# One core's adapter kernel: sixteen transposes and a whole down product in a row, gathers a group further ahead, one of four A copies on VectorE, A loaded in 512-byte runs

## The chip, the cores and the metric

The kernel runs on one core of a Trainium2 chip. The metric is the device time of one execution in microseconds (us). The kernel before has a median of 96.18 us over three runs (95.92 to 96.72).

## The reference

`x` holds 64 sequences of 64 tokens with 1024 features, in float32. Each sequence names one of 8 adapters (`itok_B_3_7`). An adapter has a `B` of 16 x 1024 (rank by features) and an `A` of 1024 x 16. What is computed:

```python
B_sel = B[adapter_ids]                       # 64 x 16 x 1024
A_sel = A[adapter_ids]                       # 64 x 1024 x 16
Bx    = einsum('bni,bri->bnr', x, B_sel)     # down to rank 16
out   = einsum('bnr,bor->bno', Bx, A_sel)    # up to 1024
return x + out * 1.0
```

So 16.8 MB are read, 16.8 MB are written, and between them every token goes through its sequence's two small products.

## The kernel before, in words

**Tiles and groups.** A tile is 128 tokens (two sequences) by 1024 features. A duo is two tiles, so four sequences, and there are 16 duos. All 32 tiles of x have a place of their own in SBUF (`x_all`), where the result is added in place and stored from. SyncE (SP) issues the load of A, then all loads of x, then the stores in order of tiles. ScalarE issues the loads of B and of the ids.

**Start.** TensorE (PE) does 24 transposes of an identity, then transposes B (L195). ScalarE (ACT) copies it into `b_table` (L287), which has for every adapter and chunk of 128 features a 128 x 16 block. A is split into a rounded part and a rest by VectorE (DVE; L338, L341, L344) and ACT (L294, L296), transposed on PE (`a_unit`, L212) and copied into `a_table` (L306, L348).

**A duo's work.** `transpose_unit` (L221) turns four 128 x 128 chunks of x into one PSUM bank; there are four units in a duo, and ACT copies each into `x_t` (`copy_x`, L301). `down` (L234) multiplies each of the eight chunks with the adapter's block for four sequences, into the 128 rows of a `bx_bank`. ACT rounds the result into `bx_parts` (`split_high`, L316), DVE writes the rest beside it (`split_rest`, L355), and GpSimd (POOL) copies both to the lower 64 rows (`double_parts`, L169). `up` (L254) multiplies that with the adapter's A into `y_banks`, and DVE adds the product to x (`add_x`, L363).

**The gathers.** Which block of the tables a sequence needs is known only at run time. POOL reads the ids into registers (L141) and copies the four blocks of B (`gather_b`, L151) and the four of A (`gather_a`, L162) of each duo into `b_duo` and `a_duo`, which have two buffers each.

**Order.** Every engine has its list written out by hand, and semaphores tie the lists together. PE's loop over the duos is: two transpose units of the next duo, the first half of this duo's down product (chunks 0 to 3), the two other units, the second half, then the up product of the duo before. Transposes use two PSUM banks, down products two, and up products four. In POOL's list a duo has: registers, B of the next duo, A of this one, `double_parts` of this one. The wait for `parts_done` ahead of the B copies is for POOL's own copy just before them.

Of the kernel before, what the change touches and what calls it, by code (L numbers as in the profile page):

```python
# [8 lines left out]
def lora_kernel(nc: bass.Bass, x: bass.AP, ids: bass.AP, a_in: bass.AP, b_in: bass.AP, out: bass.AP):  # L9
# [21 lines left out]
    A_BY_DVE = (0, 2, 4, 6)  # L31
    B_HOME, A_HOME, PARTS_HOME = TILES - 1, TILES - 2, TILES - 6
    B_OWN = CHUNKS * RANK
    WARM_UPS = 24

# [7 lines left out]
    with ctx:  # L43
# [24 lines left out]
        t_bank = [pb(f"t_bank{i}", [P, BANK]) for i in range(2)]  # L68
        bx_bank = [pb(f"bx_bank{i}", [P, BANK]) for i in range(2)]
# [18 lines left out]
        a_gathered = sem("a_gathered")  # L88
# [22 lines left out]

        def own_tokens(duo, first_row, end_row):
# [18 lines left out]
        def _(pool):  # L131
# [8 lines left out]
            def adapters_of(duo):  # L140
                return nc.values_load_multi_w_load_instructions(  # L141
                    id_row[0:1, duo * DUO_SEQS:(duo + 1) * DUO_SEQS], engines=[pool.engine],
                    min_val=0, max_val=ADAPTERS - 1,
                    skip_runtime_bounds_check_because="the ids are indices of the adapters")[1]

            def gather_b(duo, adapters):
# [8 lines left out]
                last.then_inc(b_gathered, 1)  # L155

            def gather_a(duo, adapters):
# [6 lines left out]
                last.then_inc(a_gathered, 1)  # L164
# [8 lines left out]
            here = adapters_of(0)  # L173
            gather_b(0, here)
            for duo in range(DUOS):
                if duo + 1 < DUOS:
                    after = adapters_of(duo + 1)
                    gather_b(duo + 1, after)
                if duo == 0:
# [208 lines left out]
```

## Time and profile before

| | |
|---|---|
| median of three runs | 96.18 us (95.92 to 96.72) |
| profiled execution, device time | 96.29 us |
| its span in the profile | 94.4 us |
| PE busy | 81.5 us (86%) |
| POOL busy | 67.1 us (71%) |
| DVE busy | 58.4 us (62%) |
| ACT busy | 53.1 us (56%) |
| DMA | 34.83 MB, 369 GB/s over the span |

The span runs from the first to the last recorded piece of work. The device time of the same execution is 1.9 us longer. Busy shares are means over a start, a long middle and an end with different limits, so the rows further below are read by stage. PEld is PE's loading of weights, which overlaps its multiplications, and SPq is SyncE's issuing of DMAs.

### The profile page before, as it was taken

Reading aid. Unit: us, or ns where it says so; the run is one execution under the profiler, and the core shown is the slowest. Engines: PE = TensorE matmul, PEld = TensorE weight load, DVE = VectorE, ACT = ScalarE, POOL = GpSimd, SP = SyncE. Lnnn points to the kernel's source line nnn. Section 1 sums busy time; section 2 is a strip of 40 time slices with the busy share of each in tenths; the row PEclk is TensorE's granted clock in tenths of the full one; section 3 lists DMA queues with packets and bytes.
Section 4 is the critical chain, followed back from the end, with each engine's and each line's share of the span. In section 5 each row is a group of like instructions: output and inputs, shape, how many; then the busy total and the mean of one; then the engine's idle time right before and its main releaser. Section 6 shows DMA issues by size and latency. Waiting matters only on the chain.

```text
span 94.4 us, 3723 instructions
## 1 busy us (share of the span) xinstructions
PE 81.5 (86%) x1472; PEld 64.5 (68%) x1472; DVE 58.4 (62%) x105; ACT 53.1 (56%) x138; POOL 67.1 (71%) x152
## 2 busy tenths in 40 slices
PE   3994999999999999899999999999989999652800
PEld 3993998787786768587877787777767877440400
DVE  0009541219696949396969677685857695949760
ACT  2219687985747475657667676757556757110000
POOL 6003906379798999979797979797979798986000
PEclk9999999999999999999999999999999999975555
DMA  1999999999999999999999999999999998664676
GB/s 19 305 294 394 419 417 408 408 408 412 401 413 406 408 403 403 410 412 403 408 413 408 419 403 415 417 412 415 417 410 419 410 380 327 271 266 198 247 318 252
DMA packets 11202, 34.83 MB, mean 369 GB/s; under 512 B 2866, under 2 KB 2866, under 8 KB 11186
## 3 DMA queue, kind: packets, MB, share of 16 engines
q1 hardware_dynamic: 11040, 34.08, 91.7%
q10 hardware_dynamic: 146, 0.52, 1.6%
q8 instruction: 11, 0.18, 0.7%
q14 instruction: 5, 0.04, 0.1%
HBM read 17.83 MB, written 16.78 MB: 367 GB/s over the span
## 4 chain that ended last, share of the span: by engine, by line
PE 69%; POOL 9%; DMA 7%; issue 5%; DVE 4%; POOLq 2%; DVEq 1%
PE t_bank L221 31%; PE bx_bank L234 18%; PE y_banks L254 16%; POOL a_duo L162 7%; DMA x_all<-in_A 7%; PE y_banks L212 4%; DVE x_all L363 1%; DVE x_all L341 1%; POOL b_duo L151 1%; DVEq L43 1%; DVE x_all L338 1%; DVE x_all L344 1%; POOL bx_parts L169 1%; POOLq L43 0%; POOLq L162 0%
## 5 line engine op out<-in xcount | busy, mean ns | idle before, releaser
L363 DVE TENSOR_TENSOR x_all<-y_banks,x_all 128x1024 f32<-128x1024 f32 x32 | 39.1, 1224 | 18.7 <-PE y_banks L254 18.2
L301 ACT COPY x_t<-t_bank 128x512 f32<-128x512 f32 x64 | 34.4, 591 | 19.5 <-PE t_bank L221 19.5
L162 POOL CAST a_duo<-a_table 128x512 fp32r x64 | 36.6, 609 | 3.4 <-ACT a_table L306 3.2
L221 PE MATMUL t_bank<-ident,x_all 128*128 128x128 f32 x256 | 34.9, 279 | 1.3 <-DMA x_all<-in_x 1.2
L221 PEld LDWEIGHTS t_bank<-ident,x_all 128*128 128x128 f32 x256 | 27.5, 141 | 7.8 <-issue 4.9
L151 POOL COPY b_duo<-b_table 128x256 f32 x64 | 23.2, 403 | 11.1 <-ACT b_table L287 6.2
L254 PE MATMUL y_banks<-a_duo,bx_parts 64*128 64x512 f32 x128 | 20.8, 445 | 4.0 <-POOL bx_parts L169 3.5
L234 PE MATMUL bx_bank<-x_t,b_duo 128*32 128x64 f32 x1024 | 21.7, 222 | 1.1 <-issue 0.6
L234 PEld LDWEIGHTS bx_bank<-x_t,b_duo 128*32 128x32 f32 x1024 | 16.2, 109 | 7.1 <-issue 6.2
L254 PEld LDWEIGHTS y_banks<-a_duo,bx_parts 64*128 64x128 f32 x128 | 12.0, 197 | 7.5 <-issue 3.5
L355 DVE TENSOR_TENSOR bx_parts<-bx_bank,bx_parts 32x64 fp32r<-32x64 f32 x64 | 14.0, 219 | 4.8 <-ACT bx_parts L316 3.7
L316 ACT CAST bx_parts<-bx_bank 32x64 fp32r<-32x64 f32 x64 | 13.0, 204 | 3.8 <-PE bx_bank L234 3.2
L169 POOL CAST bx_parts<-bx_parts 64x256 fp32r<-64x256 f32 x16 | 6.3, 396 | 5.1 <-DVE bx_parts L355 3.2
L190 PE MATMUL t_bank<-ident 128*128 128x128 f32 x24 | 4.7, 384 | 1.5 <-POOL ident L134 1.5
L190 PEld LDWEIGHTS t_bank<-ident 128*128 128x128 f32 x24 | 4.5, 209 | 1.5 <-POOL ident L134 1.5
L338 DVE CAST x_all<-x_all 128x512 fp32r<-128x512 f32 x2 | 0.8, 424 | 7.0 <-DMA x_all<-in_A 7.0
L348 DVE CAST a_table<-y_banks 128x512 fp32r<-128x512 f32 x4 | 2.8, 692 | 2.2 <-PE y_banks L212 2.2
L212 PE MATMUL y_banks<-ident,x_all 128*128 128x128 f32 x32 | 3.8, 273 | 0.2 <-DVE x_all L344 0.2
L212 PEld LDWEIGHTS y_banks<-ident,x_all 128*128 128x128 f32 x32 | 3.5, 140 | 0.5 <-issue 0.5
L287 ACT COPY b_table<-t_bank 128x512 f32<-128x512 f32 x2 | 1.1, 588 | 3.6 <-PE t_bank L195 3.6
L306 ACT CAST a_table<-y_banks 128x512 fp32r<-128x512 f32 x4 | 2.3, 586 | 1.2 <-PE y_banks L212 1.2
L287 ACT ACT_TABLE_LOAD x1 | 1.3, 1283 | 1.8 <-issue 1.8
(13 smaller groups left out, 7.4 us busy)
## 6 DMA issues: line engine op xcount, KB each, us to landing
out_y<-x_all SPq DMA_DIRECT2D x32, 512.0 KB, 12.4
x_all<-in_x SPq DMA_DIRECT2D x15, 1024.0 KB, 18.8
x_all<-in_x SPq DMA_DIRECT2D x2, 512.0 KB, 6.0
x_all<-in_B ACTq DMA_DIRECT2D x1, 512.0 KB, 4.1
x_all<-in_A SPq DMA_DIRECT2D x1, 512.0 KB, 6.2
id_row<-in_ids ACTq DMA_DIRECT2D x1, 0.2 KB
```

Source lines behind the costliest of these rows:

```text
L151: last = nc.gpsimd.tensor_copy(b_duo[duo % 2][:, k, :, :].rearrange("p c (e r) -> p c e r", e=2), b_table[:, bass.ds(adapters[k] * B_OWN, ...
L162: last = nc.gpsimd.tensor_copy(a_duo[duo % 2][:, k, :], a_table[:, bass.ds(adapters[k] * BANK, BANK)])
L169: nc.gpsimd.tensor_copy(own_tokens(duo, K_UP, 2 * K_UP), own_tokens(duo, 0, K_UP)).then_inc(parts_done, 1)
L190: nc.tensor.transpose(t_bank[0][:, 0:P], ident[:, :], ident[:, :])
L212: last = nc.tensor.transpose(filled[:, :, j], part_rows, ident[:, :])
L221: last = nc.tensor.transpose(t_bank[unit % 2][:, c * P:(c + 1) * P], x_all[:, 2 * duo + tile, at:at + P], ident[:, :])
L234: last = nc.tensor.matmul(bx_bank[duo % 2][k * QUAD:(k + 1) * QUAD, 0:SEQ], b_duo[duo % 2][:, k, c, :], x_t[duo % 2][:, c, tile, s * SEQ:( ...
L254: last = nc.tensor.matmul(y_banks[tile][:, h * BANK:(h + 1) * BANK], bx_parts[duo % 2][ranks, k, :], a_duo[duo % 2][ranks, k, :], start=(s ...
L301: nc.scalar.copy(x_t[duo % 2][:, half * HALF:(half + 1) * HALF, tile, :], t_bank[unit % 2][:, :].rearrange("p (c n) -> p c n", c=HALF)).th ...
L316: last = nc.scalar.copy(bx_parts[duo % 2][0:QUAD, k, s * SEQ:(s + 1) * SEQ], bx_bank[duo % 2][k * QUAD:(k + 1) * QUAD, 0:SEQ])
L355: last = nc.vector.tensor_tensor(bx_parts[duo % 2][QUAD:K_UP, k, cols], bx_bank[duo % 2][k * QUAD:(k + 1) * QUAD, 0:SEQ], bx_parts[duo % 2 ...
L363: nc.vector.tensor_tensor(here, y_banks[tile][:, :], here, ALU.add).then_inc(y_drained, 1)
```

## The change

- `adapters_of` becomes a helper that any engine may call. DVE copies the last of a duo's four A blocks (a new `gather_a` of its own, with its own load of one id register), POOL the other three.
- POOL gathers B two duos ahead and A one duo ahead of `double_parts`, and the B copies no longer wait for `parts_done`.
- PE does all four transpose units in a row and then all eight chunks of the down product. Transposes have three banks and down products one; the last duo's down product goes into a transpose bank.
- From the second duo on, the down product waits for the rest copies of the duo before.
- DVE adds both tiles of the duo before after the rest copies of a duo, and then copies its A block.
- A is loaded as one run of 512 bytes per partition and adapter, not as two of 256. Its 1024 outputs then lie in another order in the product, which `add_x` undoes by reading PSUM in runs of four numbers.

```diff
-        t_bank = [pb(f"t_bank{i}", [P, BANK]) for i in range(2)]
-        bx_bank = [pb(f"bx_bank{i}", [P, BANK]) for i in range(2)]
+        t_bank = [pb(f"t_bank{i}", [P, BANK]) for i in range(T_BANKS)]
+        bx_bank = pb("bx_bank", [P, BANK])
...
+        def own_bx(duo, k):
+            bank = t_bank[(B_UNITS + UNITS * duo + 1) % T_BANKS] if duo == DUOS - 1 else bx_bank
+            return bank[k * QUAD:(k + 1) * QUAD, 0:SEQ]
...
-            sp.dma_start(a_nat.rearrange("p a h j r -> p (a h) (j r)"),
-                         a_in.rearrange("a (h p j) r -> p (a h) (j r)", h=HALVES, j=J)).then_inc(a_loaded, 16)
+            sp.dma_start(a_nat.rearrange("p a h j r -> p a (h j r)"),
+                         a_in.rearrange("a (p h j) r -> p a (h j r)", h=HALVES, j=J)).then_inc(a_loaded, 16)
...
+            def gather_b(duo):
+                adapters = adapters_of(pool, duo * DUO_SEQS, (duo + 1) * DUO_SEQS)
                 if duo >= 2:
                     pool.wait_ge(bx_done, duo - 1)
-                    pool.wait_ge(parts_done, duo - 1)
...
             def gather_a(duo, adapters):
+                if duo >= 1:
+                    pool.wait_ge(parts_done, duo)
                 if duo >= 2:
                     pool.wait_ge(y_filled, 2 * (duo - 1))
-                    pool.wait_ge(parts_done, duo)
-                for k in range(DUO_SEQS):
+                for k in OWN_BY_POOL:
...
             def double_parts(duo):
+                pool.wait_ge(a_gathered_pool, duo + 1)
+                pool.wait_ge(b_gathered, min(duo + 3, DUOS))
                 pool.wait_ge(rest_done, duo + 1)
-                pool.wait_ge(a_gathered, duo + 1)
...
+            here = gather_b(0)
+            after = gather_b(1)
+            pool.wait_ge(a_copied_act, len(A_BY_ACT))
+            pool.wait_ge(a_copied_dve, len(A_BY_DVE))
+            gather_a(0, here)
             for duo in range(DUOS):
+                here = after
+                if duo + 2 < DUOS:
+                    after = gather_b(duo + 2)
+                double_parts(duo)
                 if duo + 1 < DUOS:
-                    after = adapters_of(duo + 1)
-                    gather_b(duo + 1, after)
...
+                    gather_a(duo + 1, here)
...
-            def down(duo, first, end):
-                if first == 0:
-                    pe.wait_ge(b_gathered, duo + 1)
-                    if duo >= 2:
-                        pe.wait_ge(rest_done, duo - 1)
-                pe.wait_ge(t_copied, B_UNITS + UNITS * duo + (3 if end <= HALF else 4))
-                for c in range(first, end):
+            def down(duo):
+                pe.wait_ge(b_gathered, duo + 1)
+                if 1 <= duo < DUOS - 1:
+                    pe.wait_ge(rest_done, duo)
+                pe.wait_ge(t_copied, B_UNITS + UNITS * (duo + 1))
+                for c in range(CHUNKS):
...
                 if duo + 1 < DUOS:
-                    transpose_unit(duo + 1, 0)
-                    transpose_unit(duo + 1, 1)
-                down(duo, 0, HALF)
-                if duo + 1 < DUOS:
-                    transpose_unit(duo + 1, 2)
-                    transpose_unit(duo + 1, 3)
-                down(duo, HALF, CHUNKS)
+                    for unit in range(UNITS):
+                        transpose_unit(duo + 1, unit)
+                down(duo)
                 if duo:
                     up(duo - 1)
...
             def add_x(duo, tile):
                 dve.wait_ge(y_filled, 2 * duo + tile + 1)
-                here = x_all[:, 2 * duo + tile, :]
-                nc.vector.tensor_tensor(here, y_banks[tile][:, :], here, ALU.add).then_inc(y_drained, 1)
-
-            split_rest(0)
-            for duo in range(1, DUOS):
-                add_x(duo - 1, 0)
+                here = x_all[:, 2 * duo + tile, :].rearrange("n (p h j) -> n p h j", h=HALVES, j=J)
+                product = y_banks[tile][:, :].rearrange("n (h p j) -> n p h j", h=HALVES, j=J)
+                nc.vector.tensor_tensor(here, product, here, ALU.add).then_inc(y_drained, 1)
+
+            def gather_a(duo):
+                k = duo * DUO_SEQS + OWN_BY_DVE
+                adapter = adapters_of(dve, k, k + 1)[0]
+                if duo >= 2:
+                    dve.wait_ge(y_filled, 2 * (duo - 1))
+                nc.vector.tensor_copy(a_duo[duo % 2][:, OWN_BY_DVE, :],
+                                      a_table[:, bass.ds(adapter * BANK, BANK)]).then_inc(a_gathered_dve, 1)
+
+            dve.wait_ge(ids_loaded, 16)
+            dve.wait_ge(a_copied_act, len(A_BY_ACT))
+            dve.wait_ge(a_copied_dve, len(A_BY_DVE))
+            gather_a(0)
+            for duo in range(DUOS):
                 split_rest(duo)
-                add_x(duo - 1, 1)
+                for tile in range(2):
+                    if duo:
+                        add_x(duo - 1, tile)
+                if duo + 1 < DUOS:
+                    gather_a(duo + 1)
```

Three places of the engines' lists show what moves. Lines are those of either kernel's own source.

On PE in the middle of the loop, before (from the up product of one duo to the next):

```order
L254 MATMUL y_banks<-a_duo,bx_parts 128x512 x8
L221 MATMUL t_bank<-ident,x_all 128x128 x8
L234 MATMUL bx_bank<-x_t,b_duo 32x64 x16
L221 MATMUL t_bank<-ident,x_all 128x128 x8
L234 MATMUL bx_bank<-x_t,b_duo 32x64 x16
L254 MATMUL y_banks<-a_duo,bx_parts 128x512 x8
```

And the same place with the change:

```order
L263 MATMUL y_banks<-a_duo,bx_parts 128x512 x8
L232 MATMUL t_bank<-ident,x_all 128x128 x16
L244 MATMUL bx_bank<-x_t,b_duo 32x64 x32
L263 MATMUL y_banks<-a_duo,bx_parts 128x512 x8
```

The instructions are the same, and two changes from one kind of matmul to the other are gone.

On POOL, one duo of the kernel before with the waits (ISA rows compute the address of the copy behind them from a register):

```order
L169 COPY bx_parts<-bx_parts 64x2x2x64 [waits a_gathered,rest_done]
L141 TENSOR_LOAD id_row
L151 ISA [waits parts_done,bx_done]
L151 COPY b_duo<-b_table 128x256
...
L162 ISA [waits parts_done,y_filled]
L162 COPY a_duo<-a_table 128x512
L162 ISA
L162 COPY a_duo<-a_table 128x512
L162 ISA
L162 COPY a_duo<-a_table 128x512
L162 ISA
L162 COPY a_duo<-a_table 128x512
```

And with the change:

```order
L178 COPY bx_parts<-bx_parts 64x2x2x64 [waits rest_done,b_gathered,a_gathered_pool]
L170 ISA [waits y_filled,parts_done]
L170 COPY a_duo<-a_table 128x512
L170 ISA
L170 COPY a_duo<-a_table 128x512
L170 ISA
L170 COPY a_duo<-a_table 128x512
L120 TENSOR_LOAD id_row
L157 ISA [waits bx_done]
L157 COPY b_duo<-b_table 128x256
```

One of the four A copies is gone, and the register load now stands between the A copies and the B copies and no longer between `double_parts` and a wait for it.

On DVE, one duo of the kernel before:

```order
L355 TENSOR_TENSOR bx_parts<-bx_bank,bx_parts 32x64 [waits high_done]
L355 TENSOR_TENSOR bx_parts<-bx_bank,bx_parts 32x64 x3
L363 TENSOR_TENSOR x_all<-y_banks,x_all 128x1024 [waits y_filled] x2
```

And with the change:

```order
L361 TENSOR_TENSOR bx_parts<-bx_bank,bx_parts 32x64 [waits high_done]
L361 TENSOR_TENSOR bx_parts<-bx_bank,bx_parts 32x64 x3
L370 TENSOR_TENSOR x_all<-y_banks,x_all 128x1024 [waits y_filled] x2
L120 TENSOR_LOAD id_row
L377 ISA [waits y_filled]
L377 COPY a_duo<-a_table 128x512
```

DVE has a register load, an address computation and a copy more. In the list of before the two additions behind the rest copies are the second tile of one duo and the first of the next; with the change both are of one duo.

## Rows read from the trace of the kernel before

**Rows 1.** Busy us by stage (instructions), then granted clock, DMA share, GB/s.
```profile
2.40:4.70 2.30, 2.30 (x13) 2.30 (x12) 0.00 (x0) 0.65 (x1) 0.00 (x0) 1.00 0.98 307
4.70:7.10 2.40, 2.40 (x19) 2.16 (x17) 0.10 (x1) 0.40 (x1) 0.00 (x0) 1.00 1.21 295
15.00:75.50 60.50, 59.33 (x1215) 46.24 (x1216) 40.80 (x76) 40.74 (x111) 51.94 (x115) 1.00 1.03 410
75.50:94.40 18.90, 10.11 (x172) 6.80 (x170) 12.34 (x20) 3.98 (x14) 10.26 (x22) 0.72 0.70 281
```

**Rows 2.** The chain that ended last, in time: start us, us, what; duos 0 and 7.
```profile
14.21 0.87 PE t_bank L221 x8
...
20.64 1.12 PE y_banks L254 x7
...
48.79 1.02 PE t_bank L221 x8
49.82 0.58 PE bx_bank L234 x32
...
52.01 1.12 PE y_banks L254 x8
```

**Rows 3.** POOL's timeline: start us, us, line, tiles, count, [idle before <-releaser].
```profile
60.40 0.40 POOL L169 CAST bx_parts<-bx_parts 64x256 fp32r<-64x256 f32 x1
61.19 1.43 POOL L151 COPY b_duo<-b_table 128x256 f32 x4 [0.40 <-POOL bx_parts L169]
62.57 2.28 POOL L162 CAST a_duo<-a_table 128x512 fp32r x4
64.99 0.40 POOL L169 CAST bx_parts<-bx_parts 64x256 fp32r<-64x256 f32 x1
```

**Rows 4.** The end's timeline: up products, A copies behind `double_parts`, last additions.
```profile
79.28 1.20 PE L254 MATMUL y_banks<-a_duo,bx_parts 64*128 64x512 f32 x8
...
83.82 2.28 POOL L162 CAST a_duo<-a_table 128x512 fp32r x4 [0.23 <-POOL bx_parts L169]
...
87.54 2.07 PE L254 MATMUL y_banks<-a_duo,bx_parts 64*128 64x512 f32 x8 [1.92 <-POOL bx_parts L169]
...
88.79 2.35 DVE L363 TENSOR_TENSOR x_all<-y_banks,x_all 128x1024 f32<-128x1024 f32 x2 [0.56 <-PE y_banks L254]
```

**Rows 5.** The timeline of duo 0's steps between its down and its up product.
```profile
17.34 0.85 ACT L316 CAST bx_parts<-bx_bank 32x64 fp32r<-32x64 f32 x4
...
18.22 0.92 DVE L355 TENSOR_TENSOR bx_parts<-bx_bank,bx_parts 32x64 fp32r<-32x64 f32 x4 [3.72 <-ACT bx_parts L316]
...
19.21 0.40 POOL L169 CAST bx_parts<-bx_parts 64x256 fp32r<-64x256 f32 x1 [1.92 <-DVE bx_parts L355]
```

**Rows 6.** Groups by line: count | busy us, mean ns | idle before, and its releaser.
```profile
L363 DVE TENSOR_TENSOR x_all<-y_banks,x_all 128x1024 f32<-128x1024 f32 x32 | 39.1, 1224 | 18.7 <-PE y_banks L254 18.2
L301 ACT COPY x_t<-t_bank 128x512 f32<-128x512 f32 x64 | 34.4, 591 | 19.5 <-PE t_bank L221 19.5
L338 DVE CAST x_all<-x_all 128x512 fp32r<-128x512 f32 x2 | 0.8, 424 | 7.0 <-DMA x_all<-in_A 7.0
```

**Rows 7.** Single lines by source: duration ns min/median/max, first and last start us.
```profile
L141 POOLq TENSOR_LOAD <-id_row x16: 317/428/684, 7.9 to 78.8; - x16
L151 POOL COPY b_duo<-b_table x64: 393/395/639, 8.6 to 80.4; 128x256 f32 x64
```

**Rows 8.** The timeline of the start, where DVE, ACT and POOL meet.
```profile
7.68 1.29 DVE L341 TENSOR_TENSOR x_all<-x_all 128x512 fp32r<-128x512 f32 x2
8.59 3.24 POOL L151 COPY b_duo<-b_table 128x256 f32 x8 [6.19 <-ACT b_table L287]
8.70 0.63 ACT L296 CAST x_all<-x_all 128x512 fp32r<-128x512 f32 x1
9.00 0.50 DVE L344 CAST x_all<-x_all 128x512 fp32r<-128x512 f32 x1
9.65 1.94 PE L212 MATMUL y_banks<-ident,x_all 128*128 128x128 f32 x16 [0.24 <-DVE x_all L344]
```

More of the change, by code:

```diff
@@ L110, in a_row, with adapters_of @@
             return a_table[:, a * BANK:(a + 1) * BANK]
+        def own_bx(duo, k):
+            bank = t_bank[(B_UNITS + UNITS * duo + 1) % T_BANKS] if duo == DUOS - 1 else bx_bank
+            return bank[k * QUAD:(k + 1) * QUAD, 0:SEQ]
+        def adapters_of(engine, first, end):
+            return nc.values_load_multi_w_load_instructions(
+                id_row[0:1, first:end], engines=[engine.engine], min_val=0, max_val=ADAPTERS - 1,
+                skip_runtime_bounds_check_because="the ids are indices of the adapters")[1]
         def own_tokens(duo, first_row, end_row):
@@ L138, in _ @@
             pool.wait_ge(ids_loaded, 16)
[L140 to L146, printed above, removed]
+            def gather_b(duo):
+                adapters = adapters_of(pool, duo * DUO_SEQS, (duo + 1) * DUO_SEQS)
                 if duo >= 2:
                     pool.wait_ge(bx_done, duo - 1)
-                    pool.wait_ge(parts_done, duo - 1)
                 for k in range(DUO_SEQS):
@@ L216, in transpose_unit @@
                 tile, half = unit // 2, unit % 2
+                filled = B_UNITS + UNITS * duo + unit
                 pe.wait_ge(x_loaded[LOAD_OF[2 * duo + tile]], 16)
-                pe.wait_ge(t_copied, B_UNITS + UNITS * duo + unit - 1)
+                if filled >= T_BANKS:
+                    pe.wait_ge(t_copied, filled - T_BANKS + 1)
                 for c in range(HALF):
                     at = (half * HALF + c) * P
-                    last = nc.tensor.transpose(t_bank[unit % 2][:, c * P:(c + 1) * P],
+                    last = nc.tensor.transpose(t_bank[filled % T_BANKS][:, c * P:(c + 1) * P],
                                                x_all[:, 2 * duo + tile, at:at + P], ident[:, :])
                 last.then_inc(t_filled, 1)
-            def down(duo, first, end):
-                if first == 0:
-                    pe.wait_ge(b_gathered, duo + 1)
-                    if duo >= 2:
-                        pe.wait_ge(rest_done, duo - 1)
-                pe.wait_ge(t_copied, B_UNITS + UNITS * duo + (3 if end <= HALF else 4))
-                for c in range(first, end):
+            def down(duo):
[4 more added lines that the diff above has]
+                for c in range(CHUNKS):
                     for k in range(DUO_SEQS):
                         tile, s = k // PER_TILE, k % PER_TILE
-                        last = nc.tensor.matmul(bx_bank[duo % 2][k * QUAD:(k + 1) * QUAD, 0:SEQ],
-                                                b_duo[duo % 2][:, k, c, :],
+                        last = nc.tensor.matmul(own_bx(duo, k), b_duo[duo % 2][:, k, c, :],
                                                 x_t[duo % 2][:, c, tile, s * SEQ:(s + 1) * SEQ],
                                                 start=(c == 0), stop=(c == CHUNKS - 1))
-                if end == CHUNKS:
-                    last.then_inc(bx_done, 1)
+                last.then_inc(bx_done, 1)
             def up(duo):
-                pe.wait_ge(a_gathered, duo + 1)
+                pe.wait_ge(a_gathered_pool, duo + 1)
+                pe.wait_ge(a_gathered_dve, duo + 1)
                 pe.wait_ge(parts_done, duo + 1)
@@ L301, in copy_x @@
                 nc.scalar.copy(x_t[duo % 2][:, half * HALF:(half + 1) * HALF, tile, :],
-                               t_bank[unit % 2][:, :].rearrange("p (c n) -> p c n", c=HALF)).then_inc(t_copied, 1)
+                               t_bank[(B_UNITS + UNITS * duo + unit) % T_BANKS][:, :]
+                               .rearrange("p (c n) -> p c n", c=HALF)).then_inc(t_copied, 1)
             def copy_a(a):
@@ L316, in split_high @@
                     last = nc.scalar.copy(bx_parts[duo % 2][0:QUAD, k, s * SEQ:(s + 1) * SEQ],
-                                          bx_bank[duo % 2][k * QUAD:(k + 1) * QUAD, 0:SEQ])
+                                          own_bx(duo, k))
                 last.then_inc(high_done, 1)
@@ L355, in split_rest @@
                     last = nc.vector.tensor_tensor(bx_parts[duo % 2][QUAD:K_UP, k, cols],
-                                                   bx_bank[duo % 2][k * QUAD:(k + 1) * QUAD, 0:SEQ],
+                                                   own_bx(duo, k),
                                                    bx_parts[duo % 2][0:QUAD, k, cols], ALU.subtract)
```

16 lines of the change are left out of this document (6 added, 10 removed).

## The prediction

> **What bounds the kernel now.** I read the stages first [rows 1]. From 15.0 to 75.5 us PE is busy for 59.3 of 60.5 us and the DMA engines move 410 GB/s, the most that any stage shows. After 75.5 PE is busy for 10.1 of 18.9 us and the rate is 281 GB/s. So the middle looks bound by PE, the end by something slower.
>
> The chain in order of time [rows 2] splits a duo's period on PE into its pieces. In duo 7: eight transposes 1.02 us, sixteen products of the down product 0.58, the same pair again, then the up product 1.12, so 4.33 us with the seams of 0.01. But from `up(0)` at 20.64 [rows 2] to `up(13)` at 79.28 [rows 4] there are 58.64 us in 13 periods, 4.51 each. POOL's timeline says why [rows 3]: from `double_parts` to `double_parts` it takes 64.99 - 60.40 = 4.59 us: 0.40 of its own, 0.39 of gap, 1.43 for B, 2.28 for A and some 0.14 before the next, less overlaps. POOL falls behind PE by a quarter of a microsecond per duo and, once PE's lead is used up, sets its pace. The end shows it: PE waits 1.92 us for POOL before the last up product [rows 4].
>
> **The start (A in longer runs).** While A and B come in, from 2.4 to 7.1 us, the rate is 307 and 295 GB/s, not 410 [rows 1]. DVE waits 7.0 us for A [rows 6], but A's transposes on PE, at 9.65, also need ACT's copy at L296, which ends at 8.70 + 0.63 = 9.33 [rows 8] and follows on PE's and ACT's work on B, not on A. An earlier A therefore gives 0.2 us to the chain at most, though a full microsecond to DVE. I take 0.2 (bounds 0 and 0.3).
>
> **PE's period.** No matmul is added or removed. Eight transposes behind other transposes take 0.87 us, behind a product 1.02 [rows 2]. The change turns one of two such turns of a duo into a run: 1.12 + 1.02 + 0.87 + 2 x 0.58 = 4.17, with seams 4.18 us. Bounds: 4.33 if the run saves nothing, and 4.10 if the down product's own turn goes free as well.
>
> Three new waits lie on PE. The third transpose bank: ACT copies a unit in 0.59 us [rows 6], and PE fills one in some 0.47, so the fourth unit, 1.4 us after the first begins, finds the first one's copy done at 0.5 + 0.6. Only in duo 2, where no up product stands between, is ACT still in its 0.85 us of rounding [rows 5]; I take 0.1 us once. The single `bx_bank`: the rest copies end 0.07 + 0.85 + 0.92 = 1.85 us behind the down product [rows 5], the next down product begins 1.12 + 1.89 = 3.0 us behind it, so there is 1.1 us to spare. DVE's A copy is finished a whole period before its up product.
>
> **POOL's period.** One A copy goes: (2.28 - 0.61) / 3 = 0.56 us, taking 0.61 for the first (that group's 36.6 us of busy time over 64 copies is 0.57). The register load leaves the gap behind `double_parts`, which was 0.40 with a load in it [rows 3] and 0.23 without one [rows 4]. Before the B copies the load costs nothing, since eight B copies with a load between them took 3.24 us with no gap [rows 8]. So 4.59 - 0.56 - 0.17 = 3.86 us. POOL was the pace at 4.59 and has 0.3 us to spare at 4.18.
>
> **DVE's period.** Rest copies 0.92 [rows 5], two additions 2.35 [rows 4], the new copy 0.42 by the nearest row, 128 x 512 from SBUF to SBUF [rows 6], seams 0.05: 3.75 us, so 0.43 to spare. The register load (0.32 to 0.68 us, [rows 7]) is issued while an addition of 1.2 us runs; I take it as hidden, as on POOL.
>
> DVE's copy and POOL's copies can hinder each other. The first B copy took 0.639 us where the median is 0.395 [rows 7]; it began at 8.59 while DVE read two SBUF operands until 8.97, and DVE's copy at 9.00, beside the second, took 0.50 us and not 0.42 [rows 8]. That is 0.08 to 0.24 us per meeting. I take 0.2 for both engines: POOL 4.06, DVE 3.95, still under 4.18, and bounds of 0 and the other's whole copy (0.42 for POOL, 0.40 for DVE). The Trainium skill (SBUF — State Buffer, Who interferes with whom) says that a VectorE copy in its two-port mode and a GpSimd instruction exclude each other for their whole length. By that rule POOL would be at 3.86 + 0.42 = 4.28 us and set the pace, and the sum below would be 1.3 us longer; the trace agrees that they block, though not for the whole length.
>
> **The sum.** Transposes of duo 1 begin at 14.21 - 0.2 = 14.0 [rows 2]: two runs of 0.87, down product 1.17, transposes of duo 2 1.9 + 0.1, down product 1.17, so `up(0)` begins at 20.05 to 20.1 where it was 20.64. Thirteen periods of 4.18 bring `up(13)` to 74.4, where it was 79.28. From there DVE has no gap: rounding and rest of duo 14 to 76.25, two additions 78.6, its A copy with a wait 79.15, rest of duo 15 80.1, two additions 82.45, the last two 84.85. The last up products fit in between even at the 2.07 us that the last one took in the stage of clock 0.72 [rows 4, 1]. The additions of before ended at 88.79 + 2.35 = 91.14, 3.26 us ahead of the span's end at 94.4. So the span ends at 88.1, and with the DMA queue a little fuller at 88.3. The profiled execution took 1.9 us more than its span: 90.2, against its own 96.29. The median of before is 0.1 lower, so 90.2 us stands for the median too.
>
> **Work that gets nothing.** Against the DMA engines I count no gain: they have 281 x 18.9 = 5.3 MB left at 75.5 us [rows 1], 13.0 us at 410 GB/s, so all bytes are moved at 88.5 if nothing changes at the start and at 87.2 if A's and B's stage runs at 410 (0.51 MB more in 4.7 us). This floor lies right at my compute end, which is why my range does not go below 89 (87.2 + 1.9 = 89.1).
>
> **Rivals.**
> 1. *The DMA engines become the bound* (chance 0.14). The start gains nothing from longer runs, the last bytes move at 88.5, and a finish of one microsecond comes on top (a lone last store needs 3.26 us, of which its 0.52 MB are 1.3): 89.5 + 1.9 = 91.4 us. For it: 410 GB/s without a dip for 60 us. Against it: stores are made at 1.05 MB per 4.18 us, 251 GB/s, so the backlog shrinks.
> 2. *DVE or POOL sets a pace of 4.4 us* (0.17), by the exclusion above, or by a register load that is not hidden on DVE (3.95 + 0.43 = 4.38): 13 x 0.22 = 2.9 us more, 93.1 us. Against it: additions follow each other with no gap, so DVE's instructions are fetched ahead. The Trainium skill (DMA: Bandwidth & Descriptors, Latency and other measured facts) has about 600 ns as the floor of a register load, by which this would be 4.55 us and 95.0; the trace has loads of 317 ns, under that floor.
> 3. *POOL stays the bound* (0.06): with the full 0.42 us of exclusion and the gap of 0.17 that I take as gone it needs 4.45, and duos with two meetings more: about 95.5 us, within 1%.
> 4. *The additions get slower, and the kernel with them* (0.06). `add_x` now reads PSUM in runs of four numbers from alternating banks. No row shows that. A read in runs of sixteen took 1.29 us for two of 512 elements [rows 8], against 1.22 for one of 1024 [rows 6], which fits one rate and a fixed part, so the nearest row says no cost. If runs of four halve the rate, an addition takes 2.3 us and DVE 6.0 per duo: 15 x 1.85 = 28 us more, 118 us. It decides from a DVE period of 4.65, an addition of about 1.65 us.
>
> **Chances.** My forecast 0.57, rivals 0.14, 0.17, 0.06, 0.06. Forecast's own range: 89.0 (period 4.10, cut by the floor) to 91.5 (period 4.28). The range is 89.0 to 93.6: below it I leave 0.07, above it rivals 3 and 4. About 1% is what a measurement of this kernel tells from no change. Faster by more: 0.88, within 1%: 0.06, slower: 0.06.
>
> **What would show it.** PE's rows should have runs of 16 transposes in 1.9 us and up products 4.18 us apart; POOL's idle time should come before its B copies or `double_parts`, with DVE or PE as releaser, and PE should never wait for POOL before 74 us. The B copies that meet DVE's A copy should take 0.5 to 0.6 us. DVE's additions should stay at 1.22 us, and its copy at 0.42 to 0.8. The DMA rate should stay near 410 GB/s to about 80 us, and from 2.4 to 7.1 us be over 350. I am wrong if up products lie 4.3 us apart or more with DVE or POOL as releaser, if additions are longer than 1.3 us, or if the last store lands more than 4 us behind the last addition.

## The result, and the profile after

The changed kernel takes 98.5 us (median of 4 runs, 97.95 to 98.62), against 96.3 us (95.92 to 96.72) for the kernel before: ratio 1.023, 95% interval 1.018 to 1.027. It is slower, with the whole interval above 1. Ratios and their intervals here and below leave out executions that lie over 1.5% above the fastest one of their kernel. The forecast of 90.2 us with a range to 93.6 was wrong, and its chance for slower was 0.06.

The stages of the changed kernel, with the columns of [rows 1]:

```profile
2.40:4.70 2.30, 2.30 (x13) 2.30 (x12) 0.00 (x0) 0.83 (x1) 0.00 (x0) 1.00 0.90 328
4.70:7.10 2.40, 2.40 (x13) 2.40 (x12) 0.86 (x3) 0.00 (x0) 0.00 (x0) 1.00 1.07 387
15.00:66.00 51.00, 44.43 (x940) 35.13 (x942) 34.80 (x70) 31.08 (x85) 37.94 (x83) 1.00 1.03 410
66.00:96.70 30.70, 23.04 (x466) 16.84 (x455) 23.71 (x44) 13.14 (x41) 17.06 (x37) 0.87 0.73 290
```

In the middle PE is busy for 44.4 of 51.0 us, where it was busy for 59.3 of 60.5 [rows 1]. No other engine comes near full. The chain in order of time (start us, us, what) shows what PE does in place of working. First around duo 1, then around duo 4:

```profile
20.02 0.69 PE bx_bank L244 x40
20.72 1.37 issue
22.09 0.54 PE bx_bank L244 x24
22.63 1.13 PE y_banks L263 x8
...
32.59 1.98 PE t_bank L232 x16
34.57 0.46 PE bx_bank L244 x21
35.03 0.85 issue
35.88 0.86 PE bx_bank L244 x43
36.74 1.13 PE y_banks L263 x7
...
74.64 1.13 PE y_banks L263 x8
75.76 1.98 PE t_bank L232 x16
77.75 1.03 PE bx_bank L244 x64
78.78 1.13 PE y_banks L263 x8
```

The last four rows are a clean duo: 1.13 + 1.98 + 1.03 = 4.14 us, where [rows 2] had 4.33. The other rows hold the loss. A down product stops after 40 of its 64 products, or after 21 (the profile records each of the program's 32 small multiplications as two; "products" below are records), for about a microsecond, at a point where the program has no wait at all. "issue" is idle time for which the profile knows no releaser. There are seven such pauses up to 66 us: 1.37, 0.31, 0.85, 1.14, 1.06, 1.18 and 0.44 us, the second and the last between transposes, the others inside down products. From 66 to 82 us there is none; an eighth, of 0.41 us at 85.40, lies off the chain.

What lies between them is countable. PE works again at 22.09, 28.69, 35.88, 42.00, 50.85, 56.92 and 63.54 us. From each point to the next PE's records are 256 instructions, give or take one: weight loads, multiplications and semaphore instructions together. The page's DMA part has a queue whose packets are of the kind "instruction":

```profile
q8 instruction: 11, 0.18, 0.8%
```

That is 11 packets of 16 KB. PE has some 3,060 instructions, 11.96 times 256. One such packet is found right ahead of each pause. The DMA answer for 33.4 to 34.7 us has it, the one for 34.65 to 35.85 us has none:

```profile
q8 instruction: 1, 0.02, 5.2%
```

In the packets' records this one runs from 33.52 to 34.60 us, and PE goes on at 35.88. For the seven pauses the distance from the packet's end to PE's next instruction is 1.3 to 1.4 us. So PE waits for its own instructions. The Trainium skill (Runtime: NRT & Kernel Launch, Instruction fetch mechanics) says that an engine's instructions are refilled in blocks of 16 KB, 256 instructions, over a DMA queue of the sequencer's own, and calls the cost of a block's bound mostly hidden. The trace agrees on block and queue, and has 0.3 to 1.4 us at a bound where the DMA engines are full.

The other engines do what was forecast (groups by line, columns as in [rows 6]):

```profile
L370 DVE TENSOR_TENSOR x_all<-y_banks,x_all 128x1024 f32<-128x1024 f32 x32 | 37.7, 1220 | 0.7 <-PE y_banks L263 0.3
L170 POOL CAST a_duo<-a_table 128x512 fp32r x48 | 27.8, 615 | 5.9 <-ACT a_table L312 3.4 <-POOL bx_parts L178 2.5
L157 POOL COPY b_duo<-b_table 128x256 f32 x64 | 23.6, 411 | 14.5 <-PE bx_bank L244 7.4 <-ACT b_table L292 7.0
L377 DVE CAST a_duo<-a_table 128x512 fp32r x16 | 7.8, 488 | 1.2 <-ACT a_table L312 1.1
```

Additions are as long as before [rows 6], and POOL now waits 7.4 us for PE's down product.

### The profile page after: what moved, and what is told of

It reads as the page before. It is cut to its first block, busy times and chain, and to the rows that moved or that the text cites. A ratio compares the mean times of both kernels' runs of the same rounds, so it can differ in the third digit from the quotient of the medians.

```text
span 96.7 us, 3740 instructions
## 1 busy us (share of the span) xinstructions
PE 79.6 (82%) x1472; PEld 63.8 (66%) x1472; DVE 63.6 (66%) x121; ACT 52.0 (54%) x138; POOL 59.4 (61%) x136
## 4 chain that ended last, share of the span: by engine, by line
PE 74%; issue 9%; DVE 6%; ACT 5%; DVEq 1%; POOL 1%; POOLq 0%
PE t_bank L232 31%; PE bx_bank L244 17%; PE y_banks L263 16%; PE t_bank L199 6%; DVE x_all L370 4%; PE y_banks L221 4%; ACT bx_parts L322 2%; DVE bx_parts L361 2%; DVEq L45 1%; ACT b_table L292 1%; ACT x_all L299 1%; PE t_bank L204 1%; ACT x_t L306 1%; ACT x_all L301 1%; DVE a_duo L377 0%
## 5 line engine op out<-in xcount | busy, mean ns | idle before, releaser
L306 ACT COPY x_t<-t_bank 128x512 f32<-128x512 f32 x64 | 33.0, 602 | 12.1 <-PE t_bank L232 12.1
L370 DVE TENSOR_TENSOR x_all<-y_banks,x_all 128x1024 f32<-128x1024 f32 x32 | 37.7, 1220 | 0.7 <-PE y_banks L263 0.3
L232 PE MATMUL t_bank<-ident,x_all 128*128 128x128 f32 x256 | 33.4, 278 | 1.0 <-issue 0.8
L170 POOL CAST a_duo<-a_table 128x512 fp32r x48 | 27.8, 615 | 5.9 <-ACT a_table L312 3.4
L361 DVE TENSOR_TENSOR bx_parts<-bx_bank,bx_parts 32x64 fp32r<-32x64 f32 x60 | 13.2, 220 | 18.0 <-ACT bx_parts L322 17.3
L244 PE MATMUL bx_bank<-x_t,b_duo 128*32 128x64 f32 x960 | 17.8, 221 | 5.6 <-issue 5.6
L244 PEld LDWEIGHTS bx_bank<-x_t,b_duo 128*32 128x32 f32 x960 | 14.6, 110 | 8.9 <-issue 8.9
L322 ACT CAST bx_parts<-bx_bank 32x64 fp32r<-32x64 f32 x60 | 12.2, 204 | 13.3 <-PE bx_bank L244 12.8
L263 PEld LDWEIGHTS y_banks<-a_duo,bx_parts 64*128 64x128 f32 x128 | 11.1, 192 | 6.7 <-issue 2.9
L377 DVE CAST a_duo<-a_table 128x512 fp32r x16 | 7.8, 488 | 1.2 <-ACT a_table L312 1.1
```

Source lines behind the costliest of these rows:

```text
L170: last = nc.gpsimd.tensor_copy(a_duo[duo % 2][:, k, :], a_table[:, bass.ds(adapters[k] * BANK, BANK)])
L232: last = nc.tensor.transpose(t_bank[filled % T_BANKS][:, c * P:(c + 1) * P], x_all[:, 2 * duo + tile, at:at + P], ident[:, :])
L244: last = nc.tensor.matmul(own_bx(duo, k), b_duo[duo % 2][:, k, c, :], x_t[duo % 2][:, c, tile, s * SEQ:(s + 1) * SEQ], start=(c == 0), sto ...
L263: last = nc.tensor.matmul(y_banks[tile][:, h * BANK:(h + 1) * BANK], bx_parts[duo % 2][ranks, k, :], a_duo[duo % 2][ranks, k, :], start=(s ...
L306: nc.scalar.copy(x_t[duo % 2][:, half * HALF:(half + 1) * HALF, tile, :], t_bank[(B_UNITS + UNITS * duo + unit) % T_BANKS][:, :] .rearrang ...
L322: last = nc.scalar.copy(bx_parts[duo % 2][0:QUAD, k, s * SEQ:(s + 1) * SEQ], own_bx(duo, k))
```

## The experiments

Theory F: PE's instruction blocks arrive late while the DMA engines are full, and what the other parts gain is lost at the blocks' bounds. Rivals: the pauses belong to a place in the work (a bank, a semaphore), or the gathers' new lists do the harm. "Delay" below is the time from PE's entry into a block to the start of the next block's packet, from the records of the trace.

**PE's order as before, the rest as in the change (e1).**

```diff
-                    for unit in range(UNITS):
-                        transpose_unit(duo + 1, unit)
-                down(duo)
+                    transpose_unit(duo + 1, 0)
+                    transpose_unit(duo + 1, 1)
+                down(duo, 0, HALF)
+                ...
+                down(duo, HALF, CHUNKS)
```

> The changed kernel with only PE's list as before: two transpose units, half the down product, two units, the other half, up. Everything else of the change stays. Theory F (late instruction blocks, rate): PE's instructions come in blocks of 16 KB by DMA, and while the DMA engines are saturated a block takes 6.0 to 6.8 us from one to the next, whatever the order; a duo needs 0.71 block, so periods stay at 4.3 to 4.8 us and the time is 95 to 97 us. Theory D (exposure): the late block costs only where a long row of short down products has emptied what PE holds ahead, so the split hides it as in the kernel before: periods 4.33, 91.5 to 93.5 us. Theory P (POOL or DVE changes hurt): as slow as the change, 98 to 99 us.

Measured: 100.99 us, ratio 1.046 (1.040 to 1.051). Slower than all three theories had it. The banks, and the waits that belong to them, are still those of the change. Pauses of 1.13, 1.08 and 1.86 us stand in its chain. Undoing the order does not undo the loss; it adds to it.

**The order and banks alone, in the kernel before (e2).**

> The kernel before with only PE's order, the three transpose banks and the single down bank of the change; POOL, DVE and the load of A as before. If PE's order and its stalls between instruction blocks make the loss (F or D): stalls of 1 to 1.4 us inside down products as in the changed kernel, 97.5 to 100 us. If the gathers or VectorE's part make the loss (P): about 96 us, no such stalls.

Measured: 101.52 us, ratio 1.048 (1.041 to 1.055), with pauses of 1.23, 1.49 and 0.98 us between 40 and 60 us. The loss needs neither the gathers nor the load of A. It is larger than expected.

**Hardly any stores (e3).**

```diff
-            for tile in range(TILES):
+            for tile in range(TILES - 4, TILES):
```

> The changed kernel, which leaves out the stores of all tiles but the last four, so that the DMA engines are idle once x is loaded (about 45 us). F and D: no stall inside a down product after that, periods of 4.14 to 4.2 us from then on, 92.5 to 94.5 us. If the stalls have nothing to do with DMA (PSUM banks, semaphores, the order itself): stalls of 1 to 1.4 us go on up to 65 us, 98 us.

Measured: 94.66 us (one run). Its stages, with the columns of [rows 1], while x is loaded and after it:

```profile
15.00:46.00 31.00, 27.03 (x594) 21.46 (x595) 20.59 (x41) 19.02 (x54) 23.41 (x53) 1.00 1.03 408
50.00:75.00 25.00, 25.00 (x530) 20.11 (x532) 21.18 (x42) 17.32 (x49) 21.83 (x48) 1.00 0.01 4
```

With 408 GB/s PE has the same pauses, with 4 GB/s none: 25.00 us busy of 25.00. The program on PE is word for word that of the change. Packets of instructions that came 6.0 to 8.1 us apart while x was loaded come 3.5 and 4.1 us apart once the loads are done, until PE's supply is ahead. So the delay comes from the DMA load.

**More instructions on PE, no more work (e4).**

```diff
                 down(duo, HALF, CHUNKS)
+                for n in range(32):
+                    pe.nop(f"pad{duo}_{n}")
```

> The kernel before with 32 empty instructions on PE in each duo, ahead of the up product: 214 instructions per duo in place of 182, no more work for the array. F (a block of 256 instructions per 6.1 to 6.5 us while the DMA engines are full): periods of 5.1 to 5.4 us, 101 to 106 us. D or any other: empty instructions run ahead of the array, periods stay at 4.5 to 4.7 us by POOL, 96 to 99 us.

Measured: 132.2 us (one run). This experiment misfired. The chain shows the reason, and it is not the blocks:

```profile
44.46 0.58 PE bx_bank L234 x32
45.05 2.02 issue
47.07 1.20 PE y_banks L254 x8
```

32 empty instructions hold PE up for 2.0 us in every duo, 63 ns each. It says nothing of the theory.

**At most two loads and four stores in flight (e5).** SyncE waits for the load two before, and with four semaphores for the store four before.

> The changed kernel, in which SyncE keeps at most two loads of x and four stores in flight. Theory F1: a block of PE's instructions comes late because it stands behind what is queued in the DMA engines; with a shorter queue the 3.6 to 6.4 us between PE's entering a block and the next fetch's start shrink to 2 to 3.5 us, the stalls at block bounds go, and the time is 90 to 94 us. Theory F2: only the share of busy time of the DMA engines matters, not what is queued: same delays and stalls, 97 to 100 us. If the cap leaves gaps in the DMA engines' work, the rate falls below 400 GB/s and PE waits for loads.

Measured: 102.77 us, ratio 1.067 (1.060 to 1.075). The cap leaves gaps: 313 GB/s from 7 to 30 us and 364 from 30 to 60. Delays were 2.9 to 4.9 us and once 6.7, so shorter at best by 0.8 us for a tenth of the rate. The cap still lets 4 MB be in flight (two loads of 1 MB, four stores of 0.5 MB), 10 us of work at 410 GB/s and more than any delay. So this does not show that the length of the queue has no part in the delay.

**Half the down product (e6).** This kernel leaves out every second chunk of the down product.

```diff
-                for c in range(CHUNKS):
+                for c in range(0, CHUNKS, 2):
```

> The changed kernel, which leaves out every second chunk of the down product: 64 instructions fewer on PE in each duo (119 in place of 183), everything else and the DMA load as in the change. F: PE then takes over 8 us for a block of 256 instructions, longer than the 6.0 to 6.8 us that a fetch takes, so no stall at block bounds but for a rare long fetch; periods go to what POOL and VectorE need, 3.9 to 4.1 us, and the time is 88.5 to 91.5 us, near the DMA engines' floor. If the stalls belong to places in the loop or to PSUM: they stay, and only 0.5 us per duo is saved: 91 to 92 us with stalls of 1 us.

Measured: 92.13 us (one run), with 0.11 MB of instructions in 7 packets. PE's timeline (start us, us, line, tiles, [idle before <-releaser]) and the stage from 15.0 to 75.5 us:

```profile
43.10 1.20 PE L263 MATMUL y_banks<-a_duo,bx_parts 64*128 64x512 f32 x8 [0.22 <-POOL bx_parts L178]
44.22 2.05 PE L232 MATMUL t_bank<-ident,x_all 128*128 128x128 f32 x16
46.20 0.65 PE L244 MATMUL bx_bank<-x_t,b_duo 128*32 128x64 f32 x32
47.09 1.20 PE L263 MATMUL y_banks<-a_duo,bx_parts 64*128 64x512 f32 x8 [0.23 <-POOL bx_parts L178]
```

```profile
15.00:75.50 60.50, 55.66 (x859) 43.65 (x860) 56.19 (x104) 42.54 (x123) 55.20 (x119) 1.00 1.03 411
```

No pause at any bound, with the DMA engines as full as ever (411 GB/s). Only 0.5 us of PE's work per duo is gone, but the time falls by 6.4 us. The duo's period is 3.99 us, and PE now waits for POOL's `double_parts`. I had put POOL's period at 3.86 to 4.06. VectorE has hardly any idle time in it either (56.2 of 60.5 us busy), and its A copy, forecast at 0.42, takes 0.73 us beside POOL's copies from 27 to 52 us. The last addition ends at 80.3 us, the rate is 424 GB/s from 82 to 85.5 and the span ends at 90.2, so the DMA engines set the end.

**A shift of 32 instructions (e7).**

```diff
-    WARM_UPS = 24
+    WARM_UPS = 8
```

> The changed kernel with 8 warm-up transposes in place of 24, so that every later PE instruction moves 32 places forward in the program. F: the stalls stay at the same places of the instruction stream (every 256 instructions), so in the work they come 32 instructions later than now, for example after 56 of 64 products of duo 1's down product in place of 40. If stalls belong to the work (a bank, a semaphore, a certain product) they stay after 40. The time is within 2 us of the change, 96.5 to 100 us.

Measured: 99.85 us (one run). The same down product of duo 1, in this kernel's timeline and then in the change's:

```profile
19.81 0.99 PE L244 MATMUL bx_bank<-x_t,b_duo 128*32 128x64 f32 x56
22.17 0.32 PE L244 MATMUL bx_bank<-x_t,b_duo 128*32 128x64 f32 x8 [1.36 <-issue]
```

```profile
19.95 0.77 PE L244 MATMUL bx_bank<-x_t,b_duo 128*32 128x64 f32 x40
22.09 0.54 PE L244 MATMUL bx_bank<-x_t,b_duo 128*32 128x64 f32 x24 [1.37 <-issue]
```

Sixteen products, with their weight loads 32 instructions, lie between 40 and 56. The pause sits at a place in the instruction stream, not in the work. With e3 and e6 this settles what the pauses are.

**The change once more (e8).**

> The changed kernel once more, for a second trace. If long fetches (8.9 us from one block to the next at about 45 us) are chance, they fall elsewhere or are missing, and the time differs by over 1 us; if they follow from the program, they come again within 1 us of the same places, 98 to 98.7 us.

Measured: 98.09 us (one run). All seven pauses are at the same products, and packets are within 0.7 us of their places in the first trace, the long delay at 42 us included (6.43 after 6.44 us). The delays follow from the program and are not chance.

**Packets of 2 KB (f1).** Every load of x and every store is made as two of half the features.

> The changed kernel, in which each load of x and each store is made as two, of half the features each, so that a packet carries 2 KB and not 4. If a block of PE's instructions waits behind packets that the DMA engines have taken up already, smaller ones let it through sooner: the delay from PE's entering a block to the next fetch falls from 3.6 to 4.8 us to some 2 to 3, and the time to 93 to 96 us. If the delay hangs on how full the DMA engines are and not on packets: the same delays, 98 to 100 us. If smaller packets cost rate (under 400 GB/s): slower than 99 us with PE waiting for loads.

Measured: 100.0 us, ratio 1.037 (1.031 to 1.044). Delays of 3.6 to 6.6 us, as in the change, at 389 GB/s. Smaller packets give nothing and cost rate.

**VectorE's copy given back to POOL (f2).**

```diff
-    OWN_BY_POOL, OWN_BY_DVE = (0, 1, 2), 3
+    OWN_BY_POOL = (0, 1, 2, 3)
```

> The changed kernel with VectorE's A copy given back to POOL, which copies four again; PE's order, the gathers' lookahead and the load of A as in the change. Theory F: PE's instruction blocks set the pace and VectorE's copy costs and gives nothing, 97 to 100 us with stalls at the same places of PE's instruction stream. Rival (VectorE's copy or its register load hurts): 94 to 96.5 us.

Measured: 97.99 us, ratio 1.014 (1.010 to 1.019), inside theory F's range and 1.5 us above the rival's. The same long delay (6.45 us) is in its trace, which is of an execution of 100.34 us. Giving VectorE's copy back gains about 0.9% (1.014 against 1.023), so the copy is not the main cause.

**The load of A alone (f3).** The kernel before with the 512-byte runs and the addition that goes with them.

> The kernel before with only the load of A in 512-byte runs and the addition in the matching order. The load gives at most 0.2 us, and additions stay at 1.22 us: 95.8 to 96.6 us. If fetch delays are so touchy that any small shift brings long ones (over 5 us from entering a block to the next fetch): 98 us or more with such a delay in its trace.

Measured: 96.49 us, ratio 1.000 (0.996 to 1.003). As expected, and no long delay.

**At most four loads and eight stores in flight (f4).**

> The changed kernel with at most four loads of x and eight stores in flight, twice the cap of the earlier run, which had gaps at 122 to 300 GB/s. If what is queued sets the fetch delay: 3 to 4 us, between the change's 3.6 to 4.8 and the earlier cap's 2.8 to 3.8, and 96 to 98 us. If it does not: 3.6 to 4.8 us as in the change, 98 to 99 us.

Measured: 98.5 us (one run), delays 3.6 to 4.8 us and once 6.4: the change's own numbers. With a twice larger cap there is nothing left of the effect. Whether a much shorter queue would shorten the delays was not run.

**What the position in the blocks is worth (g1, g2, g3, g5).** Four kernels with the same question. The first two drop from PE the wait for POOL's A copies, which `double_parts` includes, so that a duo has 182 instructions as before and not 183.

```diff
             def up(duo):
-                pe.wait_ge(a_gathered_pool, duo + 1)
```

> The changed kernel with PE's order as before and without PE's wait for POOL's A copies, which its wait for double_parts includes: 182 instructions per duo on PE as in the kernel before. Theory A (position of the program in the blocks): bounds fall where they fell before, stalls of 0.5 us at most, periods of 4.33 that POOL no longer stretches, 93.5 to 95.5 us, better than both. Theory B (POOL's and VectorE's new lists hurt PE): about 101 us, as with 183.

Measured: 100.42 us, ratio 1.041 (1.034 to 1.048). The version that I had hoped for is not this one, and theory A falls here: with blocks that begin within one instruction of where they did before, the chain has pauses of 0.88, 1.38 and 1.52 us, nearly as long as with 183.

> The changed kernel without that wait alone, so 182 instructions per duo with the run order. In either theory the run order leaves some 4.2 to 4.3 us for the last 196 instructions of most blocks where a fetch takes 5.2 to 6 us, so stalls of over 1 us stay: 97 to 99 us. Under 95.5 us would say that the order was never the cause, only the one instruction.

Measured: 98.26 us, ratio 1.021 (1.014 to 1.028), like the change.

> The kernel before with one empty instruction on PE per duo, so 183. Theory A: the bounds move into other places from block to block and stalls of over 1 us appear in some, 97.5 to 101 us. Theory B, or neither: at most the 0.05 us of an empty instruction per duo, 96.3 to 97.3 us.

Measured: 96.81 us, ratio 1.003 (1.000 to 1.007). Against theory A again.

> The kernel before with 8 warm-up transposes, so that all of PE's program moves 32 places against the blocks. Theory A: time changes by more than 1 us either way, 97 to 101 us more likely than faster, with stalls at other products. Theory B: 96 to 97 us.

Measured: 97.97 us (one run; the kernel before had 96.18 beside it). The time is in theory A's range, but not by theory A's way. `up(0)` begins at 22.38 us where it was 20.64 [rows 2], and from there to the end of the span both kernels take 73.8 us. The loss is all in the start: with fewer warm-ups the first eight transposes of x take 1.97 us and not 1.09. The pauses did move to other products, two of them of 0.57 and 0.51 us, but the time behind `up(0)` is the same.

**The new lists with PE's list and banks as before (h1).** PE and ACT do what they did, with two transpose banks and two down banks. POOL's and VectorE's lists and the load of A are those of the change.

```diff
-    T_BANKS = 3
...
-        bx_bank = pb("bx_bank", [P, BANK])
+        bx_bank = [pb(f"bx_bank{i}", [P, BANK]) for i in range(2)]
```

> PE's and ACT's lists and all PSUM banks as before; POOL's and VectorE's lists and the load of A as in the change. If PE's order and the single down bank are the whole cause: periods of 4.33 where POOL stretched them, stalls as in the kernel before, 93 to 95.5 us, better than both kernels. If PE, no longer held by POOL, meets the block bounds before its instructions are there: 96 to 100 us with stalls of over 0.8 us at several bounds.

Measured: 94.68 us (93.84, 94.01, 95.36 and 95.38, where the kernel before had 95.52 to 96.92 in 13 runs on the same chip). The ratio of these medians is 0.985, and by its two faster runs alone it would be 93.9 / 96.12 = 0.977; there is no interval. All four are below every run of the kernel before. Its middle, and below it that of the kernel with split order, three transpose banks and one down bank (g1):

```profile
15.00:66.00 51.00, 50.60 (x1029) 39.22 (x1018) 39.16 (x79) 34.59 (x95) 42.28 (x95) 1.00 1.03 410
```

```profile
15.00:66.00 51.00, 46.04 (x921) 35.47 (x919) 35.11 (x70) 31.33 (x84) 37.67 (x83) 1.00 1.03 410
```

Same order on PE, same gathers, same 410 GB/s, but with three and one banks PE gets 4.6 us less of its work done in 51 us. The two kernels differ in the banks and in the waits that come with them. One of these is seen directly, in g1's timeline of duo 1:

```profile
19.09 0.92 DVE L366 TENSOR_TENSOR bx_parts<-bx_bank,bx_parts 32x64 fp32r<-32x64 f32 x4 [1.77 <-ACT bx_parts L327]
...
20.08 0.20 PEld L245 LDWEIGHTS bx_bank<-x_t,b_duo 128*32 128x32 f32 x9 [1.15 <-POOL b_duo L157]
```

The second down product may only begin when VectorE has read the first one's only bank, at 20.01: 1.15 us, once. (The profile names POOL, which had long been done.) The rest of the difference stands as pauses at block bounds.

The delays themselves say where this comes from. At the six bounds from about 20 to 57 us, from the packets' records, in us:

| kernel | PE's order; banks (transpose, down) | other lists | delays |
|---|---|---|---|
| before | split; 2, 2 | old | 3.3, 3.5, 3.9, 4.0, 3.2, 3.4 |
| h1 | split; 2, 2 | new | 3.3, 3.5, 4.0, 4.1, 3.2, 3.3 |
| g1 | split; 3, 1 | new | 2.5, 4.2, 3.9, 6.0, 3.8, 6.1 |
| e1 | split; 3, 1 | new | 2.3, 4.5, 3.9, 5.9, 3.9, 6.1 |
| the change | in a row; 3, 1 | new | 4.2, 4.8, 3.6, 6.4, 3.7, 4.3 |
| f2 | in a row; 3, 1 | new, four A copies on POOL | 3.3, 4.8, 3.7, 6.5, 3.6, 4.1 |
| e2 | in a row; 3, 1 | old | 4.0, 4.7, 3.6, 6.8, 3.7, 4.2 |

Apart from f2's first, kernels with the same order and banks on PE have the same delays within 0.4 us, whatever POOL, VectorE and the load of A do. So while the DMA engines are full, the delays go with PE's own list and its waits. They also go with where a bound falls in it: the shift of e7 gives 6.4, 3.7, 4.1, 5.1, 3.8 and 6.4 us.

**POOL's new order alone (h2).**

> The kernel before with only POOL's list in the new order (B two duos ahead, A one ahead), all four A copies on POOL, everything else as before. POOL's period falls from 4.6 to some 4.4 us. If instruction blocks set no pace here: 94 to 95.5 us. If they do: 95.5 to 98 us, what POOL gives coming back as stalls.

Measured: 95.4 us, ratio 0.990 (0.985 to 0.994), at the upper edge of the first range. POOL's period is 4.35 us in the middle, as expected, and the pauses are the kernel before's in kind (0.13, 0.34 and 0.57 us in the chain to 72 us).

## Why the prediction was wrong, point by point

**The step that failed** is the one of the sum that let thirteen periods follow at PE's own pace, "thirteen periods of 4.18". From `up(0)` at 22.63 to `up(13)` at 82.84 there are 60.2 us. Thirteen clean periods of 4.14 make 53.8. Of the missing 6.4, six pauses are 5.0, and the work on both sides of them took 1.4 more than it takes without a break. Another 2.6 us were lost ahead of `up(0)`, forecast at 20.05: 1.4 in duo 1's down product with its pause, 0.3 in the transposes and products ahead of it (one waits 0.21 us for ACT's copy out of a bank), and 0.8 before, since the warm-up took 0.7 us longer in this execution and no part of A's load reached the chain. Behind `up(13)` the forecast had 13.9 us to the span's end, and 13.9 it took, which is luck: the last addition ended 9.5 us after `up(13)` began and not 10.45, and the span 4.3 us behind that and not 3.45. So 6.4 + 2.6 us less some 0.5 of better periods separate 88.3 from 96.7.

**Why it could not hold.** From one block's bound to the next the change took 6.6, 7.2, 6.1, 8.9, 6.1 and 6.6 us while the DMA engines were full, 6.9 in the mean. A block is 1.40 duos of 183 instructions. At 4.14 us per duo PE has used one up in 5.8 us. Before, 1.41 duos of 4.33 were 6.1 us, and a delivery (the delay, and 2.4 us from the packet's start to PE's next instruction) took 5.5 to 6.9 us at the nine bounds from 20 to 70 us. So even with the deliveries of before a block used up in 5.8 us would have met bounds that were late by up to 1.1 us (an estimate from these numbers). The change's own deliveries are longer still. That the kernel before stood at this edge was there to read: its chain has pauses of 0.12, 0.31 and 0.29 us inside down products. I took them for noise, and put the whole surplus of the period, 4.51 against 4.33, on POOL. No rival of mine had PE short of instructions, and none of my signs of being wrong looks for it: up products were up to 5.6 us apart, but with "issue" ahead of the late ones and neither DVE nor POOL.

**What was right.** PE's clean period, 4.18 forecast and 4.14 measured, though two errors cancel in it: sixteen transposes took 1.98 us and not 1.89, the down product 1.03 and not 1.17. POOL's period (3.86 to 4.06, and 3.99 in e6). The additions stayed at 1.22 us, so rival 4's condition did not occur. VectorE's copy took 0.43 us in the median and at most 0.81; its register load never showed in PE's waits, and the longest B copy was 0.585 us. Rival 2, in which POOL or VectorE sets the pace, and the Trainium skill's rule of exclusion beside it, did not decide. The load of A: a rate of 387 GB/s from 4.7 to 7.1 us where it was 295, and no gain (f3).

**What was mis-sized.** The DMA engines' floor. Where nothing else held the kernel back (e6), they ran at 411 GB/s and ended at 90.2 us of span, 92.1 us of time. My likeliest time of 90.2 lay below that, and rival 1's 91.4 was nearly right.

**Which edit did it.** Set side by side, as ratios to the kernel before:

| PE's order | banks (transpose, down) | gathers | ratio | kernels |
|---|---|---|---|---|
| split | 2, 2 | new | 94.68 / 96.12 us = 0.985 (0.977 by two runs) | h1 |
| split | 3, 1 | new | 1.041 and 1.046 | g1, e1 |
| in a row | 3, 1 | new | 1.021 and 1.023 | g2, the change |
| in a row | 3, 1 | old | 1.048 | e2 |

The new lists of POOL and VectorE, with the load of A, gain 1.5 to 2.3% by themselves, as forecast in kind; POOL's order alone gains 1.0% (h2). The row of sixteen transposes with eight chunks, on the same banks, is 2% better than the split order, also as forecast in kind. What turns the gain into a loss is the third transpose bank bought with the second down bank, some 6% in the split order (g1 against h1), of which I had counted 0.1 us and "1.1 us to spare". The row order with two and two banks was not run, so for that order the price of the banks is argued and not shown. The third bank, the single down bank and their waits always came together, so no run says which of them does it. One direct wait of 1.15 us is shown for the split order. That the rest comes as longer deliveries at block bounds is shown. Why banks and waits lengthen these deliveries, in the same way in every run, stays open: no run here shows the moment at which a block is asked for.

## What to carry to other kernels

- Count an engine's instructions against its blocks. Where an engine uses up 256 instructions faster than a block arrives under the kernel's own DMA load, the arrival of blocks is the bound, and a denser list gives less than its work says; fewer instructions help (half the down product saved 0.5 us of work per duo and 6.4 us of time). How long a block takes is no constant: with nearly the same list it was 5.5 to 6.9 us or up to 8.9.
- An "issue" pause in the middle of a group without waits, even one of 0.3 us, is a sign to follow up before any gain on that engine is forecast. Its distance to the next one in instructions tells what it is.
- Try the parts of a change apart. Here the new lists of POOL and VectorE gain and the new banks lose, and the kernel with the new lists alone is the fastest of those that compute the whole result, at 94.68 us. The row order gains 2% on the new banks; on the old ones it was not tried.

## What the runs showed of the hardware that I had not expected

- A block of PE's instructions needs about 1.0 us of transfer and 1.3 to 1.4 us more before PE goes on, and its packet starts 2.3 to 6.8 us after PE's entry into the block before while the DMA engines run at 410 GB/s. With the loads done and no stores (e3) it was 0.2 to 1.1 us at five of six bounds and 2.2 us at one.
- These delays repeat from the first trace of the change to the second (e8) within 0.1 us at the six bounds from 22 to 57 us. In the table above they agree within 0.4 us, but for one, between kernels with the same order and banks on PE, and differ by up to 2.9 us between kernels with the same order and other banks and waits (h1 and g1).
- 32 empty instructions in a row on PE cost 2.02 us, 63 ns each (e4), and none of it was hidden behind the matmuls ahead of them. One per duo cost 0.0 to 0.7% of the kernel's time (g3).
- A product of the down group takes 16 ns with its weight load (64 in 1.03 us), and a transpose 0.12 us. So a down product eats PE's instructions about eight times as fast.
